# Graph attention and aggregation on one core: the normalised rows turned by DMA instead of by TensorE

## What is computed

```python
def _L0_gnn_ref(h, adj, W):
    Wh = h @ W.T
    norms = jnp.linalg.norm(Wh, axis=1, keepdims=True)
    sim = Wh @ Wh.T / (norms * norms.T + 1e-08)
    mask = (adj > 0) | jnp.eye(N, dtype=bool)
    alpha = jax.nn.softmax(jnp.where(mask, sim, -jnp.inf), axis=1)
    return alpha @ Wh

def _L1_gnn_ref(x, adj, W_self, b_self, W_nb, b_nb, W_comb, b_comb):
    mask = (adj > 0).astype(x.dtype)
    agg = mask @ x / jnp.maximum(jnp.sum(mask, axis=1, keepdims=True), 1.0)
    combined = jnp.concatenate([x @ W_self + b_self, agg @ W_nb + b_nb], axis=-1)
    return jax.nn.relu(combined @ W_comb + b_comb)

x = _layernorm(x + _L0_gnn_ref(x, adj, L0_gnn_W), axis=-1)
x = _layernorm(x + _L1_gnn_ref(x, adj, ...), axis=-1)
```

## Time and profile before

| | |
|---|---|
| time, median of 3 runs | 935.16 us (934.76 to 936.41) |
| span of the profiled execution, first to last instruction | 932.6 us |
| TensorE busy | 905.0 us, 97% |
| VectorE busy | 607.4 us, 65% |
| ScalarE busy | 418.3 us, 45% |
| GpSimd busy | 65.5 us, 7% |
| share of the DMA queue of SyncE in 16 engines | 44.6% |

### The profile page before, as it was taken

The page is one execution under the profiler, slowest core; times in us unless marked ns, Lnnn a source line. Parts: engine busy times, 40 slices in busy tenths (PEclk is TensorE's granted clock), DMA queues, the critical chain, the costliest instruction groups (busy, mean ns, idle before and its releaser), DMA issues.

```text
span 932.6 us, 21584 instructions
## 1 busy us (share of the span) xinstructions
PE 905.0 (97%) x7231; PEld 721.2 (77%) x7231; DVE 607.4 (65%) x1262; ACT 418.3 (45%) x701; POOL 65.5 (7%) x175
## 2 busy tenths in 40 slices
PE   7989999999999999999999999989899999999996
PEld 6857777777777777777777777668678888888885
DVE  2787786978767886688778788898443333333333
ACT  4955655656556655656656565550111011111110
POOL 2300000000000000000000000002110000000000
PEclk9999999999999999999999999999999999999998
DMA  8245554555545555565565575533131330330300
GB/s 260 69 158 160 153 155 143 148 158 149 161 142 159 173 155 159 140 189 145 164 186 143 164 256 163 165 117 131 68 131 38 118 125 29 118 124 24 122 28 17
DMA packets 113346, 126.03 MB, mean 135 GB/s; under 512 B 39105, under 2 KB 90594, under 8 KB 112130
## 3 DMA queue, kind: packets, MB, share of 16 engines
q1 hardware_dynamic: 113202, 125.10, 44.6%
q0 software_dynamic: 80, 0.13, 0.1%
HBM read 100.03 MB, written 25.18 MB: 134 GB/s over the span
## 4 chain that ended last, share of the span: by engine, by line
issue 88%; PE 5%; POOL 5%; DVE 1%; POOLq 1%; DMA 0%; ACT 0%; DVEq 0%; SPq 0%
PE ps L975 3%; POOL rstd L481 3%; POOL var_eps L479 1%; PE ps L987 1%; DMA feat_lo<-xT 0%; PE ps L1021 0%; DVE work L747 0%; POOLq L480 0%; ACT prob_hi L546 0%; DVE work L637 0%; POOLq L478 0%; DVE feat_hi L680 0%; DVE big L629 0%; DVE mix_extremes L706 0%; POOLq L483 0%
## 5 line engine op out<-in xcount | busy, mean ns | idle before, releaser
L1070 PE MATMUL ps<-feat_hi,prob_hi 128*128 128x257 f16 (+1 forms) x1024 | 279.8, 273 | 0.0
L1072 PE MATMUL ps<-feat_hi,prob_lo 128*128 128x257 f16 (+1 forms) x1024 | 279.4, 273 | 0.0
L1071 PE MATMUL ps<-feat_lo,prob_hi 128*128 128x256 f16 (+1 forms) x1024 | 278.9, 272 | 0.0
L1166 PE MATMUL ps<-big,mgroup 128*128 128x257 f16 x1024 | 227.9, 273 | 1.5 <-DVE big L819 1.5
L1167 PE MATMUL ps<-big,mgroup 128*128 128x256 f16 x1024 | 227.8, 273 | 0.0
L763 DVE SCALAR_TENSOR_TENSOR prob_lo<-work,prob_hi 128x512 f16<-128x512 f32 x256 | 175.9, 687 | 76.3 <-ACT prob_hi L546 73.8
L546 ACT ACTIVATE prob_hi<-work 128x512 f16<-128x512 f32 x256 | 154.6, 625 | 88.4 <-DVE work L756 48.7
L540 ACT ACTIVATE work<-ps 128x512 f32<-128x512 f32 x144 | 84.9, 592 | 142.4 <-PE ps L1008 124.9
L551 ACT ACTIVATE mask<-work 128x1024 fp8e4<-128x1024 f32 x128 | 133.6, 1043 | 0.0
L747 DVE SCALAR_TENSOR_TENSOR work<-adj_sb,work 128x512 f32<-128x512 int32 x144 | 99.2, 689 | 34.2 <-ACT work L540 29.1
L1071 PEld LDWEIGHTS ps<-feat_lo,prob_hi 128*128 128x128 f16 x1024 | 100.3, 98 | 27.2
(11 more groups left out here) (112 smaller groups left out, 825.0 us busy)
## 6 DMA issues: line engine op xcount, KB each, us to landing
adj_sb<-adjT SPq DMA_DIRECT2D x128, 512.0 KB, 3.9
mask_spill<-mask SPq DMA_DIRECT2D x128, 128.0 KB, 2.8
mgroup<-mask_spill SPq DMA_DIRECT2D x8, 2048.0 KB, 8.3
feat_lo<-xT SPq DMA_DIRECT2D x8, 512.0 KB, 5.5
xres<-x SPq DMA_DIRECT2D x8, 512.0 KB, 5.5
x_spill<-rows SPq DMA_DIRECT2D x8, 512.0 KB, 4.6
xres<-x_spill SPq DMA_DIRECT2D x32, 128.0 KB, 2.4
out<-rows SPq DMA_DIRECT2D x32, 128.0 KB, 1.7
```

Source lines behind the costliest of these rows:

```text
L1070: pe.matmul(acc(D + 1), prob_hi[:, s, cols], feat_hi[:, jb, 0:D + 1], start=start, stop=False)
L1071: pe.matmul(acc(D), prob_hi[:, s, cols], feat_lo[:, jb, :], start=False, stop=False)
L1072: return pe.matmul(acc(D + 1), prob_lo[:, s, cols], feat_hi[:, jb, 0:D + 1], start=False, stop=stop)
L1166: pe.matmul(agg_ps(q, D + 1), lhsT, x1_hi_of(jb // GB)[:, jb % GB, 0:D + 1], start=(jb == 0), stop=False)
```

## The change

TensorE turns nothing in the opening stage. SyncE issues, for every group, half and block, one transposing DMA from `unit` straight into the score table: 64 DMAs of 128 rows x 256 columns of fp16. Two semaphores, one for each place in the ring, count them. ScalarE's unit_heads waits for the DMAs of the group before last, where it had waited for the transposes. TensorE and VectorE wait for the same counts where they had waited for or made the evictions. The identity in fp16, both evictions and the PSUM space for them are gone, and TensorE projects all eight groups in a row. On SyncE turn 0 stands between load_xT(5) and load_xT(6), turn 1 between load_xT(6) and load_xT(7), turn 2 behind load_xT(7), and turns 3 to 7 behind the two adjacency loads, ahead of the store of the norms.

```diff
@@ block.sync
+            def turn_units(g):
+                sync.wait_ge(unit_ready, g + 1)
+                for half, to in enumerate((unitT_hi, unitT_lo)):
+                    for b in range(GB):
+                        rows_of = g * GW + b * P
+                        sync.dma_start_transpose(to[:, :, rows_of:rows_of + P],
+                                                 unit[:, g % 2, half, b, :]).then_inc(unitT_loaded[g % 2], 16)
+
             for g in range(4, G):
                 sync.wait_ge(wh_done, g - 3)
                 load_xT(g)
+                if g > 4:
+                    turn_units(g - 5)
             load_unit(0, 1, 0, 2)
             load_unit(0, 1, 1, 3)
+            for g in range(3, G):
+                turn_units(g)
@@ block.scalar
-            def unitT_out(g):
-
-                act.wait_ge(unitT_done, g + 1)
-                act.activation(unitT_hi[:, :, g * GW:(g + 1) * GW], unitT_ps(g % 2, 0), ACT.Copy).then_inc(unitT_hi_ready, 1)
-
             def unit_heads(g):
 
                 act.wait_ge(norm_ready, g + 1)
-                wait(act, unitT_done, g - 1)
+                wait(act, unitT_loaded[g % 2], UNIT_TURNED * (g // 2))
@@ block.vector
-            def unitT_out(g):
-                dve.wait_ge(unitT_done, g + 1)
-                dve.tensor_copy(unitT_lo[:, :, g * GW:(g + 1) * GW], unitT_ps(g % 2, 1)).then_inc(unitT_lo_ready, 1)
@@ ahead of the main loop
-            unitT_out(G - 2)
+            dve.wait_ge(unitT_loaded[0], UNIT_TURNED * (G // 2))
@@ diagonal, first tile
                     if a == 0 and j == 0:
-                        unitT_out(G - 1)
+                        dve.wait_ge(unitT_loaded[1], UNIT_TURNED * (G // 2))
@@ block.tensor
-            for g in range(4):
+            for g in range(G):
                 project(g)
-            for g in range(G - 4):
-                turn_units(g)
-                project(g + 4)
-            turn_units(G - 4)
@@
-            pe.wait_ge(unitT_hi_ready, 1)
-            pe.wait_ge(unitT_lo_ready, 1)
+            pe.wait_ge(unitT_loaded[0], UNIT_TURNED)
             direct_scores(0, 0, 0, 0)
@@ ahead of the main loop
-            pe.wait_ge(unitT_hi_ready, G)
-            pe.wait_ge(unitT_lo_ready, G)
+            for i in range(2):
+                pe.wait_ge(unitT_loaded[i], UNIT_TURNED * (G // 2))
             pe.wait_ge(scales_ready, 1)
```

More of the change, by code:

```diff
@@ L150, in gnn_program @@
         ident = sb("ident", [P, P], F32)
-        ident16 = sb("ident16", [P, P], F16)
         ones = sb("ones", [P, P], F32)
@@ L195, in wh_ps @@
             return ps[:, 2 * slot + b // 2, (b % 2) * D:(b % 2 + 1) * D]
-        def unitT_ps(slot, half):
-            return ps[:, 4 + 2 * half + slot, :].bitcast(F16).rearrange("p (k i) -> p k i", k=KD)
         def score_ps(tile):
@@ L234, in gnn_program @@
         unit_ready = sem("unit_ready")
-        unitT_done = sem("unitT_done")
-        unitT_hi_ready = sem("unitT_hi_ready")
-        unitT_lo_ready = sem("unitT_lo_ready")
+        unitT_loaded = [sem(f"unitT_loaded{i}") for i in range(2)]
         bias_wide_ready = sem("bias_wide_ready")
@@ L295, in gnn_program @@
         PHASE0_POOL = G * 3
+        UNIT_TURNED = 16 * 2 * GB
         @block.sync
@@ L442, in _ @@
             pool.memset(ident[:, :], 0.0).then_inc(consts_cleared, 1)
-            pool.memset(ident16[:, :], 0.0).then_inc(consts_cleared, 1)
             pool.memset(ones[:, :], 1.0).then_inc(ones_ready, 1)
@@ L448, in _ @@
             pool.memset(minus_half[:, :], -0.5).then_inc(ones_ready, 1)
[L449 to L452, removed]
+            pool.wait_ge(consts_cleared, 1)
+            pool.affine_select(out=ident[:, :], in_=ident[:, :], compare_op=ALU.not_equal, fill=1.0, base=0,
+                               pattern=[[-1, P]], channel_multiplier=1).then_inc(consts_ready, 1)
             pool.wait_ge(ones_ready, 2)
@@ L528, in _ @@
                     setup_out(1, mixw[:, KD:2 * KD, :].rearrange("p k n -> p (k n)"), 1, KD * D)
-                unitT_out(g - 1)
             act.wait_ge(flag_ready, 1)
@@ L556, in diagonal @@
                 exponentials(t0, f0, 0, STEP_TILES)
-                if a == 0:
-                    unitT_out(G - 1)
                 for j in range(GB):
@@ L655, in _ @@
                     widen_biases()
-                if 0 < g < G - 1:
-                    unitT_out(g - 1)
             dve.wait_ge(norm_ready, G)
@@ L977, in project @@
                 ins.then_inc(wh_done, 1)
[L979 to L989, removed]
             pe.wait_ge(w0_loaded, 16)
-            pe.wait_ge(consts_ready, 2)
-            for g in range(4):
+            pe.wait_ge(consts_ready, 1)
+            for g in range(G):
                 project(g)
-            for g in range(G - 4):
-                turn_units(g)
-                project(g + 4)
-            turn_units(G - 4)
             def direct_scores(a, jb, t, j):
@@ L1026, in _ @@
             combine(0, w_selfT_sb, 3)
-            turn_units(G - 3)
             combine(1, w_nbT_sb, 1)
-            turn_units(G - 2)
             pe.wait_ge(extremes_ready, 1)
@@ L1042, in _ @@
             direct_scores(0, 1, 1, 1)
-            turn_units(G - 1)
             pe.wait_ge(bias_wide_ready, 1)
```

## The result

The changed kernel takes 990.38 us as the median of 4 runs (989.33 to 991.22) against 935.5 us before: a ratio of 1.0588, with a 95% interval of 1.0573 to 1.0603. It is 54.9 us slower. The forecast was 979.3 us, in a range of 948 to 1084: the time lies inside it, 11.1 us above the likeliest value.

The account below looks back on a forecast made before the run. TensorE, busy for 97% of the span, was taken as the bound, so only the main loop's start moves: 97.6 us against 55.5 (+42.1) plus 2.0 of clock, +44.1 on 935.2, gives 979.3 us; range 948 to 1084.

Parts of the forecast that it names:

- Bounds: Main loop: TensorE has no slack from 55.6 us on, so its 877 us stay and only its start moves.
- What is removed: Opening: TensorE loses 8.5 us of transposes, ScalarE 8.1 and VectorE 5.5 us of evictions, all before 55.5 us.
- The price of a DMA: SyncE's queue: each transposing DMA costs 1.14 us, 0.39 of issue plus 0.75 of packets, within 0.39 to 2.8.
- The sum: Opening: start 21.6, 64 DMAs 73.0, four loads 1.6, last landing 1.4, giving 97.6 us against 55.5, or +42.1.
- The edges: Forecast's own case: price 0.7 to 2.0 us, 70 to 154 us for the turns, 948 to 1033 us, 65%.
- Rates: Transposing DMAs: at the skill's 261 GB/s, 64 KB take an estimated 0.25 us, below the issue time.
- Late loads of xT: SyncE's queue: loads of xT groups 6 and 7 wait behind turns, project(7) ends near 50 us, costing nothing.
- The ring: Two unit buffers: ScalarE's heads wait for landings of the group before last, hidden from 0.65 us a DMA on.
- The clock: Main loop's start: TensorE's matmuls run slow after idling, losing 0 to 2.9 us, taken as 2.0.
- A price below 0.5 us: Turns on SyncE: issue alone limits and the turns hide, 933.8 or 932.2 us; chance 8%.
- One after the other at 2.8 us: Turns on SyncE: transposing DMAs never overlap, +148.9 us with the clock, 1084.1 us; chance 20%.
- The third rival: Opening: xT loads behind the turns set its length at a price of 0.65, +10.7 us, 945.9 us; chance 7%.

Follow-up runs that it names:

- cols128: Changed kernel with each transposing DMA cut in two (128 columns instead of 256, 128 DMAs instead of 64, same bytes): 1069.64 us.
- ring3: Changed kernel with 16 DMAs of 128x1024, high half issued once ready, adjacency loads behind turn 3, ring of three groups: 930.78 us, 0.9962 of the kernel before.
- cols512: Changed kernel with each DMA turning 128x512 (32 DMAs instead of 64, same bytes): 949.16 us, ratio 1.0148 to the kernel before.
- ring2: ring3 with its ring of rows back at two groups, all else kept: 936.58 us, ratio 1.0022 to the kernel before.
- kept_busy: Changed kernel with 34 matmuls of unused result added on TensorE just ahead of the main loop: 986.09 us.
- cols1024: Changed kernel with 16 DMAs of 128x1024, score tables laid out by group, loads ahead of the turns: 941.14 us, ratio 1.0067 to the kernel before.

## Why the prediction was right, and where it was off

The direction and the place held, and so did the mechanism: SyncE's chain of turns sets the start of the main loop. The price of one turn was too small, and it was made up of the wrong parts. A row for that price, SyncE's queue in the changed kernel from 72 to 92 us with 16 turns issued (packets, MB, share):

```profile
q1 hardware_dynamic: 4352, 0.99, 24.1%
```

- **Bounds.** The main loop was to stay at 877 us and only its start to move. It moved by 53.5 us (55.6 to 109.1), the slow clock added 2.2, and all that follows 0.4: together the 56.1 us between the spans.
- **What is removed** was worth nothing on the path: 128 transposes and 16 evictions are gone, but from 21.75 us on the path is SyncE's queue, on which none of them lay.
- **The price of a DMA** is the term that was mis-sized. I took 1.14 us, as an issue of 0.39 plus packets of 0.75. Measured are 1.25 us of issue and 0.04 between two. The packets hide behind the issue, as cols128 shows with half the bytes at the same price. They are also cheaper than the 47 ns of the earlier trace rows, where a packet held 540 bytes on average and not 256. In the row above they took 0.241 x 16 x 20 us / 4352 = 18 ns each, 0.3 us a DMA. So it was luck that the sum came near: the issue was 0.90 us too small, and 0.75 us of packets that do not belong in the sum stood in for it. What was left is 0.15 us, or 64 x 0.15 = 9.6 us. The row of a plain issue is no lower bound near the truth for another kind of instruction.
- **The sum** gave the last landing at 97.6 us; it came 11.4 us later, at 109.0. Of these 9.6 are the price, 1.2 a few stretched issues (the longest 2.36 us), 0.8 the loads between the turns, and 0.15 the start, less 0.3 for the last landing.
- **The edges** of the forecast's own case were not quite what its prices give. What it calls 70 to 154 us "for the turns" are times of the last landing, and 0.7 us a DMA gives 21.6 + 44.8 + 3.0 = 69.4 us, thus 949 and not 948 us.
- **Rates.** By the 261 GB/s of the Trainium skill ("DMA: Bandwidth & Descriptors", Latency and other measured facts) the issue would bind and not the data, and that half of the estimate holds. From 256 columns (64 KB, landed in 2.4 us) to 2048 (512 KB, in 4.4) 448 KB more took 2.0 us, about 229 GB/s. With turns alone in flight, back to back at 1024 columns (ring3, 42 to 48 us), the DMA engines moved 183 GB/s while the queue's packets took 115% of the 16 engines' time (packets overlap, so the share can pass 100%). That is short of 261.
- **The 1309 ns** for 128x128 in the Trainium skill ("VectorE: DVE Perf Modes", The three transpose paths) I had argued against as a figure to multiply. cols128 issues one 128x128 every 1.27 us, near that figure. It is to be multiplied, but by the number of DMAs and not by the area: 128x1024 costs an issue of 1.23 to 1.34 too.
- **Loads between turns**: 0.47 to 0.58 us instead of 0.39; the landing of the last, 1.1 us beyond its issue instead of 1.4.
- **Late loads of xT** were put at nothing, and that nearly held: with all loads ahead of the turns the main loop starts 0.5 us earlier. Of the 1.6 us between the two spans another 0.5 is a clock that rose sooner, and 0.6 lies behind the first summation. project(7) ended at 53.6 instead of near 50 us.
- **The ring** was to be covered from 0.65 us a DMA (5.2 us a group) on. ScalarE waits 47.4 us for landings, and the turns still run back to back, as in cols512 with 5.2 us a group. Below, at 2.6 us a group, it binds, which ring2 and ring3 show. The condition was in the prediction; in my expectation for 1024 columns I forgot it.
- **The clock** was put at 2.0 us of 0 to 2.9 and measured 2.2.
- **The signature**: turns of 9.1 us a group were forecast, 10.3 came; a start near 98 us, 109.1 came; first matmuls slower than 379 ns, they took 590 to 634. TensorE was to stand idle for some 40 us; it did so for 54.6 of the 87 us, in pieces, 13.6 of them ahead of the main loop.
- **The rivals.** A price below 0.5 us needed the plain issue time, and the trace shows 1.17 as the least. One after the other at 2.8 us is out: the next is issued 1.29 us after the last, although each lands after 2.4. The third rival, the late loads as the limit, needed a price of 0.65.

## What to carry to other kernels

Count a transposing DMA of 128 fp16 rows by the instruction, about 1.3 us on the queue that issues it, whatever its width up to 128x1024. Lay out source and destination so that one of them moves as much as possible before moving anything off TensorE. Once the issue is out of the way, the landing of 2.4 to 4.4 us wants a ring deep enough that no engine waits for it: here two groups lost 0.22% and three won 0.38% against the kernel that turned on TensorE.

## What the runs showed of the hardware that I had not expected

- The issue of a transposing DMA took a median of 1.23, 1.25, 1.27 and 1.23 us for the high half at 128, 256, 512 and 1024 columns of 128 rows, and 1.92 us at 2048. What the time is spent on was not found.
- At 128 columns it is no back-pressure from the DMA engines: they were at 12.6% in cols128, with the same issue. At 1024 columns this is not shown: in ring3, back to back, the queue's share was 115%, the issues took 1.33 and 1.40 us, and a landing a median of 4.0 us against 3.2 in cols1024.
- TensorE's clock was granted at 0.50 (1.2 GHz) after the idle opening of the changed kernel and back at 1.00 (2.4 GHz) some 4 us into the main loop. In kept_busy 34 matmuls that nobody needed brought it up beforehand.
